# Three score halves and one output projection bank in the cross attention of a decoder layer

## What is computed

```python
qh = split_heads(x @ Wq)                # 8 heads, 2048 queries, 128
kh = split_heads(context @ Wk)          # 8 heads, 2048 keys, 128
vh = split_heads(context @ Wv)
sim = einsum('hid,hjd->hij', qh, kh) * 128 ** -0.5
mean = sim.mean(-1)
attn = softmax((sim - mean) * 1.5 + mean)
out = einsum('hij,hjd->hid', attn, vh)
y = merge_heads(out) @ Wout + bout      # added to x
```

## Time and profile before

| what | value |
|---|---|
| runs | 1357.28, 1363.73, 1362.21 us; median 1362.21 us |
| the profiled execution | 1356.91 us, its span 1354.9 us |
| TensorE busy | 96% of the span (8358 matmuls) |
| VectorE, ScalarE, GpSimd busy | 76%, 66%, 67% |
| mean granted TensorE clock | 0.994 of full speed |
| attention loop | first scores at 396.9 us, last scores at 1186 us |

### The profile page before, as it was taken

How to read it: one execution, slowest core, us unless ns; L and a number is a source line. 1 busy time by engine, 2 the same in 40 slices (tenths; PEclk the granted TensorE clock), 3 DMA queues, 4 the chain that set the end, 5 groups by cost and what they waited for, 6 DMA issues and landing times. The chain is left out here.

```text
span 1354.9 us, 22731 instructions
## 1 busy us (share of the span) xinstructions
PE 1303.5 (96%) x8358; PEld 1068.2 (79%) x8358; DVE 1033.9 (76%) x1628; ACT 895.6 (66%) x1315; POOL 909.7 (67%) x645
## 2 busy tenths in 40 slices
PE   5999999999999999999999999999999999997998
PEld 4687788878877777777777777777777777776998
DVE  6355498769217889899898898998988989985554
ACT  4555433425655877778777778777777777776774
POOL 2544410224410999989989989989899889774553
PEclk9999999999999999999999999999999999998999
DMA  7702032246765988878878878878878878787672
GB/s 225 96 2 73 6 98 79 77 136 230 209 216 164 241 220 213 207 198 206 207 193 214 208 193 212 210 190 215 207 191 215 210 170 216 167 208 273 217 231 82
DMA packets 172377, 241.35 MB, mean 178 GB/s; under 512 B 34179, under 2 KB 78085, under 8 KB 172272
## 3 DMA queue, kind: packets, MB, share of 16 engines
q1 hardware_dynamic: 155040, 208.11, 61.0%
q10 hardware_dynamic: 15184, 25.96, 5.6%
q0 software_dynamic: 2048, 5.90, 1.1%
HBM read 64.79 MB, written 41.32 MB: 78 GB/s over the span
## 5 line engine op out<-in xcount | busy, mean ns | idle before, releaser
L1205 POOL TENSOR_TENSOR xa_pT<-xa_moved,xa_pT 128x1024 fp32r<-128x1024 f32 x246 | 585.8, 2403 | 32.4 <-ACT xa_pT L1714 29.2
L1540 PE MATMUL xa_S<-xa_kT,xa_qT 128*128 128x512 f32 x1536 | 394.8, 405 | 11.0 <-ACT xa_probs L1720 8.2
L1720 ACT ACTIVATE xa_probs<-xa_S,xa_mx_nb_rinv 128x1024 f32<-128x1024 f32 x256 | 285.9, 1117 | 170.9 <-DVE xa_mx_nb_rinv L1327 170.8
L1557 PE MATMUL xa_O<-xa_pT,xa_v 128*128 128x512 f32 x1536 | 375.9, 394 | 2.6 <-DVE xa_pT L1380 2.6
L1540 PEld LDWEIGHTS xa_S<-xa_kT,xa_qT 128*128 128x128 f32 x1536 | 284.0, 188 | 98.4 <-ACT xa_probs L1720 38.1
L1557 PEld LDWEIGHTS xa_O<-xa_pT,xa_v 128*128 128x128 f32 x1536 | 289.1, 188 | 68.1 <-DVE xa_pT L1380 2.9
L1337 DVE STREAM_TRANSPOSE xa_tq<-xa_probs 128x1024 f32<-128x1024 f32 x256 | 316.8, 1238 | 13.2 <-ACT xa_probs L1720 5.5
L1714 ACT ACTIVATE xa_pT<-xa_moved 128x1024 fp32r<-128x1024 f32 x254 | 253.8, 1049 | 1.5 <-DMA xa_moved<-xa_tq 1.2
L1322 DVE TENSOR_REDUCE xa_mx_nb_rinv<-xa_S 128x1 f32<-128x1024 f32 x128 | 155.6, 1215 | 76.8 <-PE xa_S L1540 74.5
L1324 DVE TENSOR_REDUCE xa_mxp<-xa_S 128x1 f32<-128x1024 f32 x128 | 157.5, 1230 | 16.5 <-PE xa_S L1540 16.5
L507 PE MATMUL fw_pp<-fw_hT,fw_wqk 128*128 128x512 f32 x384 | 98.0, 404 | 6.2 <-DVE fw_hT L648 4.6
(11 more groups left out here) (243 smaller groups left out, 1745.3 us busy)
## 6 DMA issues: line engine op xcount, KB each, us to landing
xa_moved<-xa_tq SPq DMA_DIRECT2D x508, 256.0 KB, 4.5
heads_k<-ci_outs SPq DMA_DIRECT2D x32, 256.0 KB, 2.0
heads_v<-ci_outs SPq DMA_DIRECT2D x32, 256.0 KB, 2.3
heads_q<-ci_outs SPq DMA_DIRECT2D x32, 256.0 KB, 2.4
xa_chunk<-heads_v ACTq DMA_DIRECT2D x32, 256.0 KB, 3.7
ex_w1s<-in_L_ffn_w_dram SPq DMA_DIRECT2D x8, 1024.0 KB, 6.8
ex_w2s<-in_L_ffn_w_dram SPq DMA_DIRECT2D x8, 1024.0 KB, 9.3
xa_chunk<-heads_q ACTq DMA_DIRECT2D x31, 256.0 KB, 3.5
```

What stands on the lines that cost most here:

```text
L1205: pool.tensor_tensor(quadrants(pT[LO], r), unit_moved(r), quadrants(pT[HI], r).bitcast(F32), ALU.subtract).then_inc(lo_ready, 1)
L1540: last = pe.matmul(S[:, k], qT[a][:, i // GT % 2, q], kT[b][h % 2][:, k * 512:(k + 1) * 512], start=(n == 0), stop=(n == 2))
L1557: last = pe.matmul(O[:], v[a][:, j * P:(j + 1) * P], pT[b][:, r % PRING, k], start=(j == 0 and n == 0), stop=(j == JT - 1 and n == 2))
L1720: act.activation(probs[:, unit % RING], S[:, 2 * u:2 * u + 2].rearrange("p a b -> p (a b)"), ACT.Exp, bias=nb[:, s % 2:s % 2 + 1], scale=S ...
```

## The change

- `S` gets six banks. From unit 12 on (`PAIRED`, the first unit of slot 6) the units of scores go round three halves (`score_banks`), and a half waits for the exponential three units back. Units 0 to 11 still use two halves, since banks 4 and 5 serve the query projections until then.
- `Y` is one bank. `out_project(g, 1)` comes two slots behind `out_project(g, 0)` instead of one, and so does the addition; each projection waits for the addition just before it. For the last three groups k = 1 uses bank 5 of S (`aside`), and their slots are those of before.
- `mxp` is gone: both maxima go to `mx` in SBUF, the router's mean to bank 3 of S (`tp[3]`), with a new wait for the context's transposes ahead of it and a new semaphore `rw_ready` ahead of the transpose that next writes that bank; the router's third small product goes to bank 4 of S.
- `pj` is a ring of four banks (O, Y, banks 4 and 5 of S).
- The load of `Wout` stands ahead of the moves of tile 7 instead of tile 5.
- `paired` is gone: copy and first addition both count on `summed`, and the three waits on it count accordingly.

```diff
@@ sums, GpSimd
-                                       tmp[:, r, 0:b - a, HB // 2:HB], ALU.add).then_inc(paired, 1)
+                                       tmp[:, r, 0:b - a, HB // 2:HB], ALU.add).then_inc(summed, 1)
                 for r in range(2):
-                    pool.wait_ge(paired, 2 * g + r + 1)
+                    pool.wait_ge(summed, 4 * g + 2 * r + 2)
@@ dot_products, VectorE
-                        dve.wait_ge(summed, 2 * g + r - 1)
+                        dve.wait_ge(summed, 4 * g + 2 * r - 2)
                         dve.wait_ge(reduced, 2 * g + r - 1)
@@ banks
+PAIRED = 2 * (LAG - 1)
-        S = ctx.enter_context(nc.psum_tensor("xa_S", [P, 4, 512], F32))
+        S = ctx.enter_context(nc.psum_tensor("xa_S", [P, 6, 512], F32))
-        Y = [ctx.enter_context(nc.psum_tensor(f"xa_Y{i}", [P, 2, D], F32)) for i in range(2)]
-        mxp = ctx.enter_context(nc.psum_tensor("xa_mxp", [P, 512], F32))
+        Y = ctx.enter_context(nc.psum_tensor("xa_Y", [P, 2 * D], F32))
-        pj = [O[:]] + [y[:].rearrange("p a b -> p (a b)") for y in Y]
+        pj = [O[:], Y[:], S[:, 4], S[:, 5]]
-            return SLOTS + OUTPUTS[g, k] if (g, k) in OUTPUTS else (g + 1) * GT + LAG + k
+            return SLOTS + OUTPUTS[g, k] if (g, k) in OUTPUTS else (g + 1) * GT + LAG + 2 * k
-            return SLOTS + SUMS[g, k] if (g, k) in SUMS else (g + 1) * GT + LAG + 1 + k
+            return SLOTS + SUMS[g, k] if (g, k) in SUMS else (g + 1) * GT + LAG + 1 + 2 * k
+        def score_banks(unit):
+            r = unit % (2 if unit < PAIRED else 3)
+            return slice(2 * r, 2 * r + 2)
@@ moves, SyncE
-                if h and i == 5:
+                if h and i == 7:
@@ maxima, VectorE
-                dve.reduce_max(mxp[:, s % 2:s % 2 + 1], S[:, 2:4].rearrange("p a b -> p (a b)"), AX) \
+                    dve.reduce_max(mx[:, u:u + 1], S[:, score_banks(2 * s + u)].rearrange("p a b -> p (a b)"), AX) \
@@ scores, TensorE
-                    if s:
-                        pe.wait_ge(exp_done, 2 * (s - 1) + u + 1)
+                    unit = 2 * s + u
+                    banks = S[:, score_banks(unit)]
+                    if unit >= 2:
+                        pe.wait_ge(exp_done, unit - 1 if unit < PAIRED + 2 else unit - 2)
@@ out_project, TensorE
-                if g:
+                if aside(g, k) and not aside(g - 1, k):
+                    pe.wait_ge(exp_done, 2 * SLOTS)
+                elif aside(g - 1, 1):
                     pe.wait_ge(y_used, 2 * (g - 1) + k + 1)
+                elif g or k:
+                    pe.wait_ge(y_used, 2 * g + k)
```

More of the change, by code:

```diff
@@ L256, in _ @@
                 sp.wait_ge(reduced, count)
-                sp.wait_ge(summed, count)
+                sp.wait_ge(summed, 2 * count)
                 for s in range(HALVES):
@@ L919, in cross_block @@
         rows_ln = sem("xa_ln")
-        rw_in, x1_out = sem("ex_rw_in"), sem("ex_x1_out")
+        rw_in, rw_ready, x1_out = sem("ex_rw_in"), sem("ex_rw_ready"), sem("ex_x1_out")
         w_in = [sem(f"ex_w_in{i}") for i in range(2)]
@@ L1315, in _ @@
             dve.wait_ge(pj_mm, KU + 1)
-            dve.tensor_tensor(rw[:], rw[:], mxp[:, 0:E].unsqueeze(1).to_broadcast([P, DC, E]), ALU.subtract)
+            dve.tensor_tensor(rw[:], rw[:], tp[3][:, 0:E].unsqueeze(1).to_broadcast([P, DC, E]), ALU.subtract) \
+                .then_inc(rw_ready, 1)
             for n in range(CTX_BANKS, CTX_BANKS + Z_BANKS):
@@ L1320, in maxima @@
             def maxima(s):
[L1321 to L1325 removed]
+                for u in range(2):
+                    dve.wait_ge(sim_done, 2 * s + u + 1)
+                    dve.reduce_max(mx[:, u:u + 1], S[:, score_banks(2 * s + u)].rearrange("p a b -> p (a b)"), AX) \
+                        .then_inc(mx_ready, 1)
                 dve.wait_ge(mx_ready, 2 * s + 2)
[L1327 removed]
+                dve.tensor_scalar(nb[:, s % 2:s % 2 + 1], mx[:, 1:2], mx[:, 0:1], -SOFT_SCALE,
                                   ALU.max, ALU.mult).then_inc(nb_ready, 1)
@@ L1478, in transposes @@
                     pe.wait_ge(tp_lo, n - 3)
+                if n == CTX_BANKS + 3:
+                    pe.wait_ge(rw_ready, 1)
                 for k in range(4):
@@ L1509, in _ @@
             pe.wait_ge(xb_ready, HALVES)
+            pe.wait_ge(tp_lo, CTX_BANKS)
             for c in range(DC):
-                pe.matmul(mxp[:, 0:E], share[:], rw[:, c], start=(c == 0), stop=(c == DC - 1))
+                pe.matmul(tp[3][:, 0:E], share[:], rw[:, c], start=(c == 0), stop=(c == DC - 1))
             for n in range(VU):
@@ L1535, in scores @@
                 for u in range(2):
-                    if s:
-                        pe.wait_ge(exp_done, 2 * (s - 1) + u + 1)
+                    unit = 2 * s + u
+                    banks = S[:, score_banks(unit)]
+                    if unit >= 2:
+                        pe.wait_ge(exp_done, unit - 1 if unit < PAIRED + 2 else unit - 2)
                     for n, (a, b) in enumerate(PARTS):
                         for k in (2 * u, 2 * u + 1):
-                            last = pe.matmul(S[:, k], qT[a][:, i // GT % 2, q], kT[b][h % 2][:, k * 512:(k + 1) * 512],
+                            last = pe.matmul(banks[:, k % 2], qT[a][:, i // GT % 2, q], kT[b][h % 2][:, k * 512:(k + 1) * 512],
                                              start=(n == 0), stop=(n == 2))
@@ L1564, in out_project @@
                     pe.wait_ge(wo_in, 16 * (g // 4 + 1))
-                if g:
+                if aside(g, k) and not aside(g - 1, k):
+                    pe.wait_ge(exp_done, 2 * SLOTS)
+                elif aside(g - 1, 1):
                     pe.wait_ge(y_used, 2 * (g - 1) + k + 1)
+                elif g or k:
+                    pe.wait_ge(y_used, 2 * g + k)
                 for m in range(2):
                     t = 2 * k + m
-                    last = pe.matmul(Y[k][:, m], oT[:, t * P:(t + 1) * P], woh[:], start=True, stop=True)
+                    last = pe.matmul(output_bank(g, k)[:, m], oT[:, t * P:(t + 1) * P], woh[:], start=True, stop=True)
                 last.then_inc(y_mm, 1)
@@ L1600, in positions, with keep_busy @@
                 pe.matmul(rp[q], ones[:], pre[:, quad(q)], start=False, stop=True).then_inc(pos_mm, 1)
-            def keep_busy(n, bank=Y[1][:, 0, 0:P]):
+            def keep_busy(n, bank=S[:, 5, 0:P]):
                 for _ in range(n):
@@ L1614, in _ @@
                     pe.wait_ge(pj_out, UNITS)
-                    keep_busy(8)
+                    keep_busy(8, Y[:, 0:P])
                 if s == SLOTS:
@@ L1719, in exponential @@
                     act.wait_ge(tr_done, unit - RING + 1)
-                act.activation(probs[:, unit % RING], S[:, 2 * u:2 * u + 2].rearrange("p a b -> p (a b)"),
+                act.activation(probs[:, unit % RING], S[:, score_banks(unit)].rearrange("p a b -> p (a b)"),
                                ACT.Exp, bias=nb[:, s % 2:s % 2 + 1], scale=SOFT_SCALE,
```

13 lines of the change are left out of this document (8 added, 5 removed).

## The result

| | before | after |
|---|---|---|
| median of four runs (lowest to highest) | 1362.97 us (1357.28 to 1364.32) | 1339.62 us (1338.53 to 1343.30) |
| ratio of the fast runs (that of the two medians is 0.983) | | 0.9841, 95% interval 0.9806 to 0.9876 |
| the profiled execution, its span | 1356.91, 1354.87 us | 1338.53, 1336.49 us |
| mean granted TensorE clock | 0.994 | 0.989 |

A forecast was written before the change was run, and what follows sets the result against it. TensorE was taken as the bound, 728.6 of 737.3 us busy in the loop, with late score starts to remove. Terms 22.1 + 1.5 + 0.5 = 24.1 us off 1360 gave 1336 us, range 1329 to 1350.

The forecast's parts named there:

- Late starts in the loop: Scores in slots 12 to 123: the third half removes their late starts, 0.79 us a group, 22.1 us in all.
- the unit of 2.75: Attention loop: twelve TensorE matmuls with nothing late take 2.75 us from start to next block's start.
- The 1.06 us: Scores' second half in the loop: its exponential is there 1.06 us before it is asked for.
- Rivals 1 and 2: Loop: GpSimd becomes the bound, 1347 us, chance 0.10; the wait moves to the scores' second half, 1358 us, chance 0.06.
- Rival 3: Output projections in the loop: k = 1 waits for the addition of k = 0, 1373 us, chance 0.04.
- Start and end: Both ends of the loop: 1.5 us off at the start, 0.5 us at the end.
- The tail: Behind the loop's last exponential: a chain that doesn't shorten, so no gain counted there.
- The output bank: Output projections: one bank costs 0 two slots apart, cover 4.0 us; without the cover 1.2 us a group.
- The load of `Wout`: SyncE's queue, two tiles later: issues in slot 25 or 26, over 8 us ahead; cost 0, bound 1 us a head.
- The two counts of `summed`: GpSimd's copy and addition on one semaphore: cost 0, bounds -0.2 and 0.5 us in all.
- The sum: Whole kernel: 22.1 + 1.5 + 0.5 = 24.1 us off.
- a base of 1360: Starting time for the sum, between the profiled execution's 1356.9 us and the median of three runs.

The follow-up runs named there:

- e1: The changed kernel with the ring of scores back at two halves, all else as changed: 1351.9 us, 0.9945 of before.
- e5: The kernel before with one more VectorE maximum over 128 scores in each slot, its result overwritten: 1382.15 us, 1.0153 of before.
- e6: The changed kernel with one more VectorE maximum over 128 scores in each slot, its result overwritten: 1341.7 us, 0.9860 of before.
- e2: The changed kernel with one output bank, but projection and addition of k = 1 one slot behind k = 0: 1376.51 us, 1.0121 of before.
- a0: The changed kernel run again, unaltered, as base for the runs beside it: 1338.31 us, 0.9830 of before.
- a1: The changed kernel run again, unaltered, as base for other runs beside it: 1340.38 us, 0.9849 of before.
- f1: The kernel before with only `paired` merged into `summed`: 1358.37 us, 0.9997 of before.
- e4: The changed kernel with the load of `Wout` back ahead of the moves of tile 5: 1335.88 us, 0.9831 of before.
- e8: The changed kernel with the load of `Wout` ahead of the moves of tile 6: 1333.88 us, 0.9816 of before.
- e9: The changed kernel with `Wout` loaded ahead of tile 6 and small unused matmuls in TensorE's waits after the loop: 1335.51 us, 0.9830 of before.

## Why the prediction was right, and where not

**Late starts in the loop: right.** 0.79 us a group were to go, 24.61 to 23.8; measured 24.63 to 23.88 (medians of the groups), 0.75. Over slots 12 to 119 (27 groups) that is 20.2 us; the stage gave 19.8, with 0.6 taken back by the late load of `Wout`, where 27 x 0.79 would be 21.3. By blocks: the two late steps of 2.98 and 3.07 became 2.77 each (0.51), and the two scores behind them went from 2.89 to 2.80 (706.36 to 709.16) where I had taken 2.75. So the unit of 2.75 was 0.05 too low for them, and 27 groups got 1.5 us less with the load's 0.6. e1 and e5 show that the wait was for the exponential behind VectorE's maxima, e6 that it has slack now. The 1.06 us by which the exponential would be early is 1.3. Nothing else came late in its place: VectorE waits 47.7 us for the scores, GpSimd's low parts hold the values' weight loads for 1.7 us in all. Rivals 1 and 2 didn't happen. Rival 3 did in e2 only, where the spacing is one slot.

**But one step was left out of it.** I gave the whole gain to the third half. The alternation of projections takes away some of the late starts by itself, 4.6 of 19.8 us by e1, and the third half the other 15.2. The prediction used that alternation only to pay for VectorE's additions. The total doesn't suffer, since both act on the same late starts.

**Start and end: right.** 1.5 us at the start was 1.3. For slots 120 to 127 the sum had 0.79 + 0.5 = 1.3 us, up to the last exponential. From slot 120's scores to the transposes that wait for it the trace has 51.9 us before and 50.2 after, 1.7 less (and 50.2 in a0 and a1). At the last scores the gain is 3.2 us, but that is the wrong place to read it: 1.5 of it is time that TensorE now waits behind them instead of in front.

**The tail.** "The tail behind the last exponential is a chain that doesn't shorten" is right, and it doesn't lengthen either: from the transposes to the experts it takes 63.7 us before (64.2 in f1), 64.2 in a0 and 64.3 in a1. But in the execution shown first it takes 65.9. The sum had no term for the clock. That TensorE stands for 2.07 us instead of 0.45 in front of the transposes follows from the change, since 1.5 us of waiting have moved from in front of the last scores to behind them; in some executions the lower clock follows, and takes back about 1 to 1.5 us.

**The output bank: right.** No wait with two slots between, and 4.3 us of cover where 4.0 were said; e2 gives the cost without the cover, 1.3 us a group against the 1.2 predicted.

**The load of `Wout`: wrong, the step that failed.** It was put at no cost with over 8 us of cover. The cover was nothing in the heads where TensorE waited and up to 1.6 us in the others. The cost of 0.1 to 0.6 us a head on the mean lies inside the bound of 1 us, that of single heads does not (1.5 us in a0, 1.8 in e6). The step named the moves *behind* the load and not those *in front* of it. Moved by two tiles, it is queued behind the moves of tile 6, and these wait for GpSimd to free the ring of three; so it issues a slot later than I said, and then takes 4.7 us to land (the median) where it took 2.9 in e4. I took over the moment of issue from a place in the queue that the load had just left.

**The two counts of `summed`: right.** f1 is 0.9997.

**The sum.** 24.1 us off was said; the loop and its ends gave 22.9 in the trace. The profiled execution fell by only 18.4, and the medians by 23.4 (1362.97 to 1339.62), since the profiled execution of before lay 6.1 us under its kernel's median, and that of after 1.1. Beside the repeats the kernel before had medians of 1362.51 and 1359.23 us, so these fell by 24.2 and 18.9. With a base of 1360, a choice between two values, the forecast was 1336; measured 1339.6, and 1338.3 and 1340.4 in the repeats. The late load (1 to 3 us), the 0.05 us a group and the clock are of the size of the 2 to 4 us between, and so is the spread of the base; the runs don't tell them apart.

## What to carry to other kernels

- When the engine at 96% still has a list of short waits for a buffer, sum the steps from start to start of its blocks: 34 us of waiting weight loads cost some 21 us here (19.8 in 27 groups, 1.7 at the end), and 8.7 us showed as idle. Another buffer removes the wait where its release is just late; shrinking a second buffer to pay for it is free if enough work stands between its uses, and e2 shows the price if not.
- An operation that is moved down an in-order queue inherits the waits of everything it is now behind. Look there for its new time of issue, and for how long the transfer takes at that place; and try the places between: the earliest one (e4) held up the moves, though at no cost that shows, and the middle one (e8) nothing.
- Where a stage ends in a chain that doesn't shorten, count the gain only up to its entrance, and cut the table at the event that starts the chain (here the last exponential): 3.2 us at the last scores were 1.7 at the entrance. The lowest median was e8's, 1333.9 us, 0.9816 of before; the intervals of e4 and e9 overlap its own.

## What the runs showed of the hardware

- The same idle time of 2.07 us on TensorE was followed by 3.4 us at 1.2 GHz in one execution (0.66 of full speed on the mean from 1169 to 1174) and by none in another (2.06 us idle, 1.00 from 1169 to 1174). Behind the same wait it fell in e4 (2.07 us) and e6 (3.20), and not in a1 and e8 (2.07). A twelve-matmul block that met it took 4.25 us instead of 3.0, one that lay wholly in a low stretch 5.49. Whether one lay over the first expert's matmuls decided between 100.4 and 101.7 us for the last stage.
- A small load on SyncE's queue landed after 2.1 to 3.2 us in one place of the loop (e4) and after 3.5 to 5.6 in another (after), with 4.3 us as the median in e8, between them.
- The time ahead of the attention loop differed by 5.2 us between executions (395.0 in e1 and e8 to 400.2 in a1), more than several of the effects studied; a stage table keeps it apart.
